# Attention kernel on one core: the transpose that feeds the row of maxima runs at key tile 1 instead of key tile 0, with a 128-column stationary operand

## The chip, the cores and the metric

One Trainium2 chip, one of its cores. The metric is the device time of one execution in microseconds, the median over several runs.

## The reference

For each of 16 sequences of 1024 tokens with 512 channels the reference adds a masked self-attention to its input:

```python
q = xt @ Wq.T                                   # 8 heads of 64 channels
scores = scale * jnp.einsum('bhqd,bhkd->bhqk', qh, qh)
logits = (scores * cmask + (1.0 - cmask) * NEG) * rmask
attn = jax.nn.softmax(logits, axis=-1)
ctx = jnp.einsum('bhqk,bhkd->bhqd', attn, qh)
out = ctx.transpose(0, 2, 1, 3).reshape(B, T, D) @ Wo.T
x = x + transpose(out)
```

Queries, keys and values are the same matrix. About half of the tokens are masked. A masked query has the same logit for every key, so its output is the mean of all tokens times both weight matrices.

## The kernel before

The kernel gathers the unmasked tokens of a sequence (a "batch" b) into NT = 5 tiles of R = 108 rows (the form "small", taken here), and does dense attention on them. For every head the 540 queries stand in two halves of H = 270 columns, and the keys in five tiles. The loops run over 16 batches (a hardware loop over pairs of batches for most of them), in each over 8 heads h, and in each over 5 key tiles k. I call one pass of the innermost loop the step (h, k). Each of the five engines has its own program with the same loops, and waits on semaphores for the others.

TensorE (`batch`, `misc`) does in the step (h, k), in this order:

1. `max_scores` 2k of head h+2 (line 1029): scores of one half of the queries against one tile, whose maxima are needed to subtract them before the exponential;
2. `scores` of head h, tile k (lines 1044 and 1047);
3. part 0 of the step's small jobs;
4. `max_scores` 2k+1 of head h+2;
5. `times_values` of the tile before (line 1057, 64 stationary columns a half);
6. part 1 of the small jobs.

The small jobs are set by tables of steps at the head of the file: V (transposes of the values), L (row sums, line 1151), proj and out (projections, line 1090), xT (transposes of the next batch's tokens, line 1102, at (3,1) to (3,4) and (4,0)), and mT. They write into two PSUM banks in turn: a job waits until the job two before it has left its bank (`bank_left`). Long jobs are split between the two parts; xT and mT are done in part 1, V and L in part 0.

The way of the maxima of head h+1 is: VectorE reduces each `max_scores` (`reduce_max`, line 831, two PSUM banks in turn), folds them into the column `mcol` at the end of head h-1 (line 836), TensorE transposes `mcol` (job mT, line 1146) in head h, ScalarE copies the result to `mrow` (`max_row`, line 655), and SyncE writes it by DMA as one row of the operands of head h+1 (`put_max_row`, line 431). TensorE's `scores` of head h+1 wait for it.

SyncE's queue (`batch` in the sync block) has two things to do in head h, in this order: `put_max_row` for head h+1, and `copy_operands` for head h+3, six DMAs (line 425) that build the operands `ops` of that head. The first `max_scores` of head h+3, at the start of head h+1, wait for these six.

ScalarE does in each step the two exponentials (line 702), then its share of the step's jobs in the order of the table (for xT the copy of line 605 and the masking of the next tile, line 675), then at key tile 1 of odd heads `ctx_high` (line 667), which feeds `ctx_low` on VectorE (line 867, at key tile 2), which the job out at step (1,2) waits for.

Of the kernel before, what the change touches and what calls it, by code (L numbers as in the profile page):

```python
# [19 lines left out]
P = 128  # L20
F32 = mybir.dt.float32
# [4 lines left out]
ALU = mybir.AluOpType  # L26
# [15 lines left out]
XT_AT = [(3, 1), (3, 2), (3, 3), (3, 4), (4, 0)]  # L42
OUT_AT = [(1, 2), (1, 4), (2, 0), (2, 2), (2, 3)]
XBAR_AT, W_AT = (7, 1), (7, 3)
RECIPROCAL_AT = [(2, 1), (2, 1), (3, 0), (3, 1)]
SCALE_AT = [(4, 1), (0, 0)]
CTX_LOW_AT = (2, 0)
# [25 lines left out]
def misc_jobs(form, has_prev, has_next):  # L73

    NT = form.NT
    table = {(h, k): [] for h in range(HEADS) for k in range(NT)}
    steps = list(table)
    for h in range(HEADS):  # L80
        if h % 2 == 1 and (h < 7 or has_next):
            table[h, V_AT[0]].append(("V", ((h + 1) // 2, 0)))
            table[h, V_AT[1]].append(("V", ((h + 1) // 2, 1)))
        if h > 0 or has_prev:
            table[h, 2].append(("L", h - 1))
    if has_prev:
        for k, at in enumerate(out_steps(form)):
            table[at].append(("out", k))

    for at, pair in zip(PROJ_AT, ((2, 1), (3, 0), (3, 1), (4, 0), (4, 1), (5, 0), (5, 1), (6, 0))):  # L90
        if at < (4, 0) or has_next:
            table[at].append(("proj", pair))
    if has_next:
        for k in range(NT):
            table[XT_AT[k] if form.split else (3, k)].append(("xT", k))
        table[XBAR_AT].append(("xbar", 0))
        table[W_AT].append(("w", 0))
    for h in range(HEADS - 1 + has_next):
        table[h, 0].append(("mT", h + 1))
    for jobs in table.values():  # L100

        assert all(name not in TWO_PARTS for name, _ in jobs[:-2])
    return table
# [126 lines left out]
def attention_kernel(nc, x_rows, mask_t, wq, wqT, woT, out_rows, B, T, D):  # L230
# [6 lines left out]
    with ExitStack() as ctx:  # L237
# [6 lines left out]
        def sem(name):  # L244
            return ctx.enter_context(nc.semaphore(name))
# [37 lines left out]
        out_step, out_done, rsum_done = sem("out_step"), sem("out_done"), sem("rsum_done")  # L283
        recip_step, xlo_done, ctx_lo_done = sem("recip_step"), sem("xlo_done"), sem("ctx_lo_done")

        wlo_done = sem("wlo_done")
        pacc_step, idx_copied, tail_added = sem("pacc_step"), sem("idx_copied"), sem("tail_added")

        sp_passed, pool_passed = sem("sp_passed"), sem("pool_passed")
# [21 lines left out]
        for f, t in zip(forms, tensors):  # L311
            own = ExitStack()

            def keep(name, shape, dt, stack=own, t=t, f=f):
                t[name] = sb(f"{f.name}_{name}", shape, dt, stack)
# [38 lines left out]
            keep("xsum", [P, D], F32)  # L354
            keep("xv", [P, f.NA, D], F32)
            keep("mxp", [P, 2, f.NT, 2], F32)
            keep("mcol", [P, 2, f.NT], F32)
            keep("mrow", [f.NT, 2, f.R], F32R)
            if f.split:
                for name in ("wqT_hi", "wqT_lo", "woT_hi", "woT_lo"):  # L360
# [93 lines left out]
        def _(pool):  # L454
# [14 lines left out]
            def body(f, t, plan):  # L469
# [84 lines left out]
                pool.wait_ge(idx_made, 2)  # L554
                if f.split:
                    pool.wait_ge(wlo_done, 2)
                nc.gpsimd.memset(t["ops"][DK:P, :, OPX, :].bitcast(F32), 0.0).then_inc(ops_cleared, 1)
                nc.gpsimd.memset(t["ops"][DK:P, :, OPY, :].bitcast(F32), 0.0).then_inc(ops_cleared, 1)
                pool.wait_ge(ops_cleared, 2)
# [173 lines left out]
        def _(dve):  # L733
# [25 lines left out]
            def body(f, t, plan):  # L759
# [68 lines left out]
                def reduce_max(s, h, m):  # L828

                    dve.wait_ge(mx_ready, 2 * NT * s + m + 1)  # L830
                    nc.vector.tensor_reduce(t["mxp"][:R, h % 2, m // 2, m % 2:m % 2 + 1], MX[m % 2][:R, 0:H], AX.X,  # L831
                                            ALU.max).then_inc(mx_red, 1)
                    if m == 2 * NT - 1:
                        dve.wait_ge(mx_red, 2 * NT * (s + 1))
                        at_least(dve, mT_ready, s - 1)
                        nc.vector.tensor_reduce(t["mcol"][:R, h % 2, :], t["mxp"][:R, h % 2], AX.X, ALU.max,
                                                negate=True).then_inc(mcol_done, 1)

                def job(name, arg, bank, b, par, s):
# [134 lines left out]
        def _(pe):  # L974
# [11 lines left out]
            def body(f, t, plan):  # L986
# [107 lines left out]
                def job(name, arg, bank, before, b, par, s, chunks=range(KD)):  # L1094
# [35 lines left out]
                    elif name == "V":  # L1130
# [11 lines left out]
                                                    start=False, stop=True)  # L1142
                        last.then_inc(v_ready, 1)
                    elif name == "mT":
                        pe.wait_ge(mcol_done, s + 1)
                        nc.tensor.transpose(mb[:NT, 0:R], t["mcol"][:R, arg % 2, :], ident[:R, :R]).then_inc(mT_ready, 1)
                    elif name == "L":

                        pe.wait_ge(pacc_step, (NT - 1) * (s + 1))
                        for half in range(2):  # L1150
                            last = nc.tensor.matmul(mb[DK * half:DK * half + DK, 0:H], ones64[:R, :],  # L1151
                                                    t["Pacc"][:R, arg % HEADS % f.NA, half, :], start=True, stop=True)
                        last.then_inc(l_ready, 1)
                    elif name == "out":
                        if chunks[0] == 0:

                            pe.wait_ge(ctx_lo_done if f.split else ctx_done, (PAIRS if f.split else HEADS) * b)
                        for c in chunks:
                            last = product(mb[:R, 0:D], "ctxT", t["ctxT"],
                                           (slice(None), c, tile_cols(arg)),  # L1160
                                           "woT", woT_sb, (slice(None), c, slice(None)), c)
                        if c == KD - 1:
                            last.then_inc(out_ready, 1)
# [77 lines left out]
```

## Time and profile before

| what | value |
|---|---|
| median of 3 runs | 1997.83 us (1994.7 to 2000.62) |
| span of the profiled execution | 2000.9 us |
| PE (TensorE matmul) | 1806.9 us busy, 90% |
| DVE (VectorE) | 1486.2 us, 74% |
| POOL (GpSimd) | 1203.5 us, 60% |
| ACT (ScalarE) | 946.8 us, 47% |
| mean granted TensorE clock | 0.956 of full speed |
| chain that ended last | PE 50%, DVE 24%, issue 16%, ACT 4%, POOL 3%, DMA 1% |

The profiled execution's span of 2000.9 us lies 0.15% above the median of the runs. The busy shares are means over stages in which different engines are late: TensorE is nearly always busy, and in some steps waits for VectorE.

### The profile page before, as it was taken

How to read it: one execution, taken by the hardware profiler on the slowest of the kernel's cores; microseconds unless marked ns; L12 is line 12 of the kernel's file. 1: busy time of each engine (PE TensorE's matmuls, PEld its weight loads, DVE VectorE, ACT ScalarE, POOL GpSimd, SP SyncE). 2: the span in 40 equal slices, each digit the busy share in tenths (PEclk: the TensorE clock that was granted, in tenths of full speed). 3: DMA queues.
4: the chain of work that ended last, by engine and by line, in shares of the span. 5: the costliest groups of instructions: out<-in, count | busy, mean ns of one | idle time of the engine just before them, and what ended most of it. 6: DMA issues, size and time to landing. Idle time of an engine off the chain costs nothing.

```text
span 2000.9 us, 39654 instructions
## 1 busy us (share of the span) xinstructions
PE 1806.9 (90%) x10636; PEld 1184.8 (59%) x10636; DVE 1486.2 (74%) x2839; ACT 946.8 (47%) x2311; POOL 1203.5 (60%) x1030
## 2 busy tenths in 40 slices
PE   6599989999999999989999999999989999998995
PEld 4456656656556565656656666566656656665663
DVE  4359687787958778697876968668696787869774
ACT  1246455454535545354544535445454554536452
POOL 5265666647566574666646566564766656576653
PEclk8689999999989999999989999889999999999997
DMA  3233343434324342343424334243343424334320
GB/s 106 50 98 91 95 98 81 122 68 115 89 71 113 69 124 65 102 101 75 113 67 115 84 91 99 64 113 78 102 101 77 111 68 117 86 93 105 78 71 24
DMA packets 93863, 179.69 MB, mean 90 GB/s; under 512 B 24704, under 2 KB 24832, under 8 KB 93632
## 3 DMA queue, kind: packets, MB, share of 16 engines
q1 hardware_dynamic: 64448, 109.71, 23.8%
q0 software_dynamic: 29184, 67.17, 12.1%
q8 instruction: 112, 1.84, 0.4%
q14 instruction: 119, 0.97, 0.2%
HBM read 36.77 MB, written 33.55 MB: 35 GB/s over the span
## 4 chain that ended last, share of the span: by engine, by line
PE 50%; DVE 24%; issue 16%; ACT 4%; POOL 3%; DVEq 1%; SPq 1%; DMA 1%; ACTq 0%; POOLq 0%
PE misc L1090 20%; PE ctx_psum L1057 9%; DVE small_mxp L831 9%; PE max_scores L1029 7%; DVE small_xsum L826 5%; DVE small_ctx L880 4%; PE scores L1044 3%; PE scores L1047 3%; PE misc L1116 3%; PE misc L1151 2%; DVE small_rsum L862 2%; DVE small_xcT_lo L854 1%; DVE small_ctxT_lo L867 1%; ACT small_H L633 1%; ACT small_Q L630 1%
## 5 line engine op out<-in xcount | busy, mean ns | idle before, releaser
L831 DVE TENSOR_REDUCE small_mxp<-max_scores 108x1 f32<-108x270 f32 x1280 | 530.8, 423 | 378.2 <-PE max_scores L1029 359.1
L539 POOL TENSOR_TENSOR small_Pacc<-small_Pacc,small_Pt 108x540 f32<-108x540 f32 x384 | 547.1, 1425 | 370.7 <-ACT small_Pt L702 366.7
L702 ACT ACTIVATE small_Pt<-scores,small_kbias 108x270 f32<-108x270 f32 x1280 | 551.0, 483 | 404.9 <-PE scores L1047 371.8
L1029 PE MATMUL max_scores<-small_ops 128*108 128x270 f32 x1280 | 457.8, 359 | 126.7 <-DVE small_mxp L831 118.4
L1057 PE MATMUL ctx_psum<-small_Pt,small_V 108*64 108x270 f32 x2560 | 448.3, 425 | 1.9 <-ACT small_ctxraw L661 1.9
L1029 PEld LDWEIGHTS max_scores<-small_ops 128*108 128x108 f32 x1280 | 225.5, 176 | 357.7 <-DVE small_mxp L831 250.3
L862 DVE RECIPROCAL small_rsum<-small_rsum 128x67 f32<-128x67 f32 (+1 forms) x512 | 271.2, 551 | 5.5 <-ACT small_rsum L648 4.2
L539 POOL TENSOR_TENSOR small_Pacc<-small_Pt 108x540 f32<-108x540 f32 x128 | 178.4, 1394 | 158.0 <-ACT small_Pt L702 156.4
L1044 PE MATMUL scores<-small_ops 128*108 128x270 f32 x1280 | 272.9, 295 | 0.0
L1047 PE MATMUL scores<-small_ops 128*108 128x270 f32 x1280 | 269.4, 292 | 0.0
L880 DVE TENSOR_TENSOR small_ctx<-small_rsum,small_ctxraw 64x270 f32<-64x270 f32 x256 | 242.8, 948 | 9.7 <-issue 0.3
L491 POOL DMA_INDIRECT small_xg<-x_rows,small_idx_cur x160 | 166.1, 1038 | 103.9 <-POOL small_idx_cur L484 69.7
L498 POOL DMA_INDIRECT out_rows<-small_xg,small_idx_cur x160 | 162.8, 1017 | 93.1 <-DVE small_xg L915 51.5
L630 ACT COPY small_Q<-misc 128x270 f32<-128x270 f32 x128 | 49.2, 384 | 334.7 <-PE misc L1090 327.8
L1044 PEld LDWEIGHTS scores<-small_ops 128*108 128x108 f32 x1280 | 196.5, 178 | 11.2 <-issue 4.9
L1057 PEld LDWEIGHTS ctx_psum<-small_Pt,small_V 108*64 108x64 f32 x2560 | 134.0, 137 | 113.3 <-issue 57.9
L1047 PEld LDWEIGHTS scores<-small_ops 128*108 128x108 f32 x1280 | 196.0, 177 | 0.0
L826 DVE TENSOR_TENSOR small_xsum<-small_xsum,small_xg 108x512 f32<-108x512 f32 (+1 forms) x128 | 180.6, 1411 | 2.0
L1090 PE MATMUL misc<-small_xcT,small_wqT_hi 128*128 128x270 f32 x512 | 163.8, 320 | 1.9 <-DVE small_xcT_lo L854 1.3
L1090 PE MATMUL misc<-small_xcT_lo,small_wqT_hi 128*128 128x270 f32 x512 | 150.8, 295 | 0.0
L1090 PE MATMUL misc<-small_woT_hi,small_ctxT 128*108 128x512 f32 x320 | 135.9, 425 | 16.3 <-DVE small_ctxT_lo L867 16.3
L1090 PE MATMUL misc<-small_xcT,small_wqT_lo 128*128 128x270 f32 x512 | 150.2, 293 | 0.0
(104 smaller groups left out, 2184.4 us busy)
## 6 DMA issues: line engine op xcount, KB each, us to landing
small_ops<-small_H SPq DMA_DIRECT2D x512, 135.0 KB, 3.2
small_ops<-small_L SPq DMA_DIRECT2D x256, 135.0 KB, 3.4
small_xg<-x_rows,small_idx_cur POOLq DMA_INDIRECT x160, 4.2
out_rows<-small_xg,small_idx_cur POOLq DMA_INDIRECT x160, 3.4
small_ops<-small_mrow SPq DMA_DIRECT2D x128, 2.1 KB
wq_sb<-wq SPq DMA_DIRECT2D x1, 1024.0 KB, 5.4
woT_sb<-woT SPq DMA_DIRECT2D x1, 1024.0 KB, 7.8
wqT_sb<-wqT SPq DMA_DIRECT2D x1, 1024.0 KB, 9.8
```

The lines of the kernel that those rows point to most:

```text
L491: nc.gpsimd.indirect_dma_start(out=t["xg"][:r, par, k, :], out_offset=None, in_=x_rows, in_offset=bass.IndirectOffsetOnAxis(ap=t["idx_cur" ...
L539: nc.gpsimd.tensor_tensor(acc, other, t["Pt"][:R, p0], ALU.add).then_inc(pacc_step, 1)
L702: nc.scalar.activation(t["Pt"][:R, (NT * h + k) % f.NP, half, :], ST[(2 * (NT * h + k) + half) % 3][:R, 0:H], ACT.Exp, bias=t["kbias"][:R, ...
L826: nc.vector.tensor_tensor(acc[:r], other, t["xg"][:r, par, k, :], ALU.add).then_inc(xsum_step, 1)
L831: nc.vector.tensor_reduce(t["mxp"][:R, h % 2, m // 2, m % 2:m % 2 + 1], MX[m % 2][:R, 0:H], AX.X, ALU.max).then_inc(mx_red, 1)
L862: nc.vector.reciprocal(t["rsum"][:, cols], t["rsum"][:, cols]).then_inc(recip_step, 1)
L880: last = nc.vector.tensor_tensor(t["ctx"][pr:pr + DK, h // 2 % 2, cols] if f.split else t["ctxT"][pr:pr + DK, h // 2, cols], t["rsum"][r0: ...
L1029: nc.tensor.matmul(MX[m % 2][:R, 0:H], ops[:, OPA, tile_cols(m // 2)], ops[:, OPB, half_cols(m % 2)], start=True, stop=True).then_inc(mx_r ...
L1044: nc.tensor.matmul(banks[half][:R, 0:H], ops[:, OPA, tile_cols(k)], ops[:, OPB, half_cols(half)], start=True, stop=False)
L1047: nc.tensor.matmul(banks[half][:R, 0:H], ops[:, OPY, tile_cols(k)], ops[:, OPX, half_cols(half)], start=False, stop=True).then_inc(s_ready, 1)
L1057: last = nc.tensor.matmul(CT[DK * half:DK * half + DK, 0:H], t["V"][:R, (h // 2) % 2, k, DK * (h % 2):DK * (h % 2) + DK], t["Pt"][:R, (NT ...
L1090: last = nc.tensor.matmul(out, lefts[a][left_at], rights[z][right_at], start=(c == 0 and i == 0), stop=(c == KD - 1 and i == 2))
```

## The change

The job mT is put into the table at key tile 1 instead of key tile 0, on all engines that read the table. `mcol` is widened from NT columns to 128, of which the last 123 are cleared once at the start by GpSimd; the transpose takes all 128 as its stationary operand and writes 128 rows of the bank instead of 5. ScalarE still reads the first 5. TensorE waits in addition for the clearing.

```diff
+MT_AT = 1
@@ misc_jobs
     for h in range(HEADS - 1 + has_next):
-        table[h, 0].append(("mT", h + 1))
+        table[h, MT_AT].append(("mT", h + 1))
@@ tensors
-            keep("mcol", [P, 2, f.NT], F32)
+            keep("mcol", [P, 2, P], F32)
@@ gpsimd, before the loops
+                nc.gpsimd.memset(t["mcol"][:, :, NT:], 0.0).then_inc(mcol_padded, 1)
+                pool.wait_ge(mcol_padded, 1)
@@ vector, reduce_max
-                        nc.vector.tensor_reduce(t["mcol"][:R, h % 2, :], t["mxp"][:R, h % 2], AX.X, ALU.max,
+                        nc.vector.tensor_reduce(t["mcol"][:R, h % 2, 0:NT], t["mxp"][:R, h % 2], AX.X, ALU.max,
@@ tensor, job
                     elif name == "mT":
+                        pe.wait_ge(mcol_padded, 1)
                         pe.wait_ge(mcol_done, s + 1)
-                        nc.tensor.transpose(mb[:NT, 0:R], t["mcol"][:R, arg % 2, :], ident[:R, :R]).then_inc(mT_ready, 1)
+                        nc.tensor.transpose(mb[:, 0:R], t["mcol"][:R, arg % 2, :], ident[:R, :R]).then_inc(mT_ready, 1)
```

## Rows read from the trace of the kernel before

**Rows 1.** Waits: engine, line, who ended it: us in total, times, longest.

```profile
PE max_scores L1029 <- DVE small_mxp L831: 118.4, 209, 5.1
...
PE misc L1090 <- DVE small_ctxT_lo L867: 16.3, 16, 4.9
```

**Rows 2.** Groups by line and shape: busy us, mean ns | idle before, releasers.

```profile
L1102 PEld LDWEIGHTS misc<-ident,small_xv 108*128 108x128 f32 x320 | 34.3, 153 | 46.6 <-issue 29.0 <-ACT small_xv L675 12.8 <-DVE small_xcT_lo L854 4.9
...
L1146 PE MATMUL misc<-ident,small_mcol 108*5 108x108 f32 x128 | 33.0, 258 | 4.2 <-DVE small_xcT_lo L854 3.5 <-DVE small_mcol L836 0.7
...
L1146 PEld LDWEIGHTS misc<-ident,small_mcol 108*5 108x5 f32 x128 | 10.7, 83 | 45.5 <-issue 39.2 <-DVE small_xcT_lo L854 4.3 <-DVE small_mcol L836 1.0
```

**Rows 3.** Timeline (start, duration), TensorE, batch 7, heads 3 and 4.

```profile
968.94 0.26 PE L1146 MATMUL misc<-ident,small_mcol 108*5 108x108 f32 x1
...
973.34 0.68 PE L1151 MATMUL misc<-small_Pacc,ones 108*64 108x270 f32 x4
...
979.65 0.35 PE L1029 MATMUL max_scores<-small_ops 128*108 128x270 f32 x1
...
981.75 0.26 PE L1146 MATMUL misc<-ident,small_mcol 108*5 108x108 f32 x1
981.78 0.36 PE L1029 MATMUL max_scores<-small_ops 128*108 128x270 f32 x1
```

**Rows 4.** Timeline, ScalarE, same head 3.

```profile
969.32 0.24 ACT L655 CAST small_mrow<-misc 5x108 fp32r<-5x108 f32 x1 [0.66 <-PE misc L1146]
...
973.31 0.72 ACT L675 ACTIVATE small_xv<-small_xg,small_valid 108x512 f32<-108x512 f32 x1
...
973.93 0.63 ACT L667 CAST small_ctxT<-small_ctx 128x540 fp32r<-128x540 f32 x1
```

**Rows 5.** Timeline, SyncE, same head: the last of the six copies.

```profile
973.96 0.60 SPq L425 DMA_DIRECT2D small_ops<-small_L  x1
```

**Rows 6.** Window just after that transfer (us, TensorE clock, DMA share, GB/s).

```profile
978.00:979.00 1.00, 1.00 0.02 8
```

**Rows 7.** All DMAs into the operands, from issue to landing.

```profile
DMA to landing us min/median/max: 2.2/3.2/6.4
```

**Rows 8.** Timeline, VectorE, in head 3 and at the start of head 4.

```profile
973.44 0.61 DVE L854 TENSOR_TENSOR small_xcT_lo<-misc,small_xcT 128x432 fp32r<-128x432 f32 x1
...
980.58 0.42 DVE L831 TENSOR_REDUCE small_mxp<-max_scores 108x1 f32<-108x270 f32 x1
```

**Rows 9.** Timeline, batch 7: ScalarE in head 0, TensorE in heads 0 and 1.

```profile
919.68 0.24 ACT L655 CAST small_mrow<-misc 5x108 fp32r<-5x108 f32 x1 [0.26 <-PE misc L1146]
...
922.61 0.37 PE L1029 MATMUL max_scores<-small_ops 128*108 128x270 f32 x1
...
929.54 0.38 PE L1029 MATMUL max_scores<-small_ops 128*108 128x270 f32 x1
```

**Rows 10.** Window after the transfer of head 0 (clock, DMA share, GB/s).

```profile
927.00:928.00 1.00, 1.00 0.02 4
```

**Rows 11.** Timeline, batch 7, head 1: ScalarE, VectorE, TensorE.

```profile
934.52 0.68 ACT L667 CAST small_ctxT<-small_ctx 128x540 fp32r<-128x540 f32 x1
...
935.67 1.20 DVE L867 TENSOR_TENSOR small_ctxT_lo<-small_ctx,small_ctxT 128x540 fp32r<-128x540 f32 x1
...
934.79 0.37 PE L1029 MATMUL max_scores<-small_ops 128*108 128x270 f32 x1
...
937.01 0.45 PE L1090 MATMUL misc<-small_woT_hi,small_ctxT 128*108 128x512 f32 x1 [0.75 <-DVE small_ctxT_lo L867]
```

**Rows 12.** Windows over head 0 of batches 4 and 5, head 3 of 10 and 11: us, PE busy, clock, DMA.

```profile
556.60:572.93 16.33, 14.59 (x67) 0.69 0.24 55
680.10:691.84 11.74, 10.74 (x70) 1.00 0.31 72
1329.93:1346.76 16.83, 15.55 (x79) 0.70 0.44 116
1448.65:1461.77 13.12, 11.46 (x78) 1.00 0.53 133
```

More of the change, by code:

```diff
@@ L284, in attention_kernel @@
         recip_step, xlo_done, ctx_lo_done = sem("recip_step"), sem("xlo_done"), sem("ctx_lo_done")
-        wlo_done = sem("wlo_done")
+        wlo_done, mcol_padded = sem("wlo_done"), sem("mcol_padded")
         pacc_step, idx_copied, tail_added = sem("pacc_step"), sem("idx_copied"), sem("tail_added")
```

## The prediction

> **What bounds the kernel now.** I read the page's busy shares first: TensorE is busy for 90% of the span, no other engine for more than 74%, and the chain that ended last lies on PE for 50% and on DVE for 24%. So TensorE's queue sets the pace, and what can hurt is what makes it wait. The table of waits says what does so today: VectorE's reductions of the maxima, 118 us in 209 waits, and at one place in each batch `ctx_low`, 16.3 us in 16 waits [rows 1]. SyncE's copies cost TensorE almost nothing. The reader is to see that both the transpose mT and the copies are off this path, and that the question is with how much room. For that I read the timeline of one whole batch (batch 7), and there four ends: where mT runs, where its `mrow` is made, when the last of the six copies behind it has landed, and when TensorE first needs them.
>
> **The transpose itself.** In 128 executions it is 33.0 us of matmul and 10.7 us of weight load, 258 and 83 ns each [rows 2], but what it takes of TensorE's time is the step to the next start: `max_scores` starts 0.03 us after it where VectorE is not late (981.75 to 981.78) [rows 3]. At key tile 0 TensorE mostly waits for VectorE afterwards, so taking it away there gives 0 to 0.03 us. At key tile 1 little waits behind it, and it costs its full price. That price with 128 columns is not in the trace; the nearest is the weight load of the 128-column transposes, 153 ns against 83 [rows 2]. So 0.03 us if the load stays covered, 0.10 if the difference of 0.07 is added, and nothing speaks for less. I take 0.045 us over the 7 heads other than head 3 in 16 batches: 112 x 0.045 = 5 us, with ends 3 and 11.
>
> The Trainium skill ("TensorE: Matmul & The Clock Gate", section "LDWEIGHTS (loading the stationary operand)") makes a load as long as its number of columns at 1.2 GHz. That would be an estimated 0.10 us more for 128 columns than for 5, and an estimated 13 us for all; the trace has a difference of 0.07 us, and by that the upper end stands.
>
> **The edits with one answer.** The clearing of 123 columns on GpSimd happens once before the loops, where SyncE and TensorE wait for the projections anyway: 0, at most 1 us. The wait on it is met for good after that and stands with two others before a weight load that starts late anyway: 0. VectorE's fold and ScalarE's copy are as long as before.
>
> **The copies behind mT.** This is the large term. On SyncE `copy_operands` stands behind `put_max_row`, which waits for `mrow`. So moving mT moves six DMAs too.
>
> Head 3 first. There ScalarE has, at key tile 1, the xT copy and the masking (from 973.31) to do ahead of the moved `max_row`, because xT stands before mT in the table. The place that comes free is where `ctx_high` starts now, 973.93; with 0.24 us `mrow` is then done at 974.17 instead of 969.32 + 0.24 = 969.56, which is 4.61 us later [rows 4]. Now the last copy is issued at 973.96 [rows 5] and the engines are quiet again by 978.0 [rows 6], 1.65 us before TensorE's first `max_scores` of head 4 at 979.65 [rows 3]. Moved by 4.61 they land at 982.61, and TensorE stands for 2.96 us. Of this a part is hidden: VectorE is behind at that place and reduces that `max_scores`, which ends at 979.65 + 0.35 = 980.00, only from 980.58 [rows 8]. That takes 0.58 off: 2.4 us. Head 3 has xT in 15 of the 16 batches: 36 us. How long a copy takes is the uncertain part: here 4.0 us from the last issue to landing, in all between 2.2 and 6.4 [rows 7], since the gathers share the engines. With 2.2 the term is 15 x 0.6 = 9 us, with 6.4 it is 15 x 4.8 = 72. I take the row of the place itself.
>
> Head 0: `mrow` is done at 919.92. Moved, mT starts close before the `max_scores` at 922.61, and `mrow` follows 0.38 + 0.24 us behind it (968.94 to 969.32 [rows 3, 4]), at 923.23: 3.31 us later [rows 9]. The copies are through by 927.0 [rows 10] and would be by 930.3, where TensorE wants them at 929.54 [rows 9]: 0.8 us, of which I estimate half to fall into the wait for VectorE that follows. Four of the even batches have a longer head 0 with room enough. 11 x 0.35 = 4 us. Heads 5 and 6 are about as long as head 0 and reach their limit by the same reckoning; I give them 3 us together, with ends 0 and 10. Heads 1, 2, 4 and 7 last clearly longer in the timeline and have the room.
>
> **What else stands behind mT.** In head 1 `ctx_high` on ScalarE, now from 934.52 for 0.68 us, comes to stand behind the moved `max_row`. With mT just before 934.79, `mrow` is done at about 935.38 and `ctx_high` at 936.06, so `ctx_low` begins 0.4 us after its 935.67 of now. The projection at 937.01 already waits for it by 0.75 us [rows 11]. So 0.4 us lies wholly on the path, in 15 batches: 6 us, and nothing covers it. In heads 5 and 7 no such job waits at that place. In head 3 a second effect is hidden: the row sums (973.34 [rows 3]) now have xT two jobs before them and wait for its bank, which VectorE's `xcT_lo` leaves at 974.05 [rows 8]. These 0.7 us come before the stall at head 4, which is shorter by the same, so they are not added.
>
> **TensorE's clock.** Head 0 takes 11.74 us in batch 5 at a granted clock of 1.00, and 16.33 in batch 4 at 0.69; head 3 takes 13.12 us in batch 11 at 1.00 and 16.83 in batch 10 at 0.70 [rows 12]. So where the clock falls to its lower level (1.2 GHz) for part of a head, that head is some 3.7 us longer, part of it the pause itself. Waits of 3 us at the start of head 4 may bring it down more often. I take 9 us (one more fall of a third of that size in half of the batches would be 9), with ends 0 and 15 x 3.7 = 56.
>
> **The sum.** 36 + 4 + 3 + 6 + 5 + 9 = 63 us on the profiled execution's 2000.9 us gives a span of 2064. The runs' median lies 3 us under that span, so 1997.8 + 63 = 2061 us.
>
> **The rivals.**
>
> 1. The copies come quickly. Shifted, they may meet fewer gathers; with 2.2 us instead of 4.0 head 3 costs 9 us, heads 0, 5 and 6 nothing, and 6 + 5 remain: 1997.8 + 20 = 2018 us. For it speaks the median of 3.2 us [rows 7], against it that gathers of the next batch run through all of head 3 and 4. Chance 0.17.
> 2. The clock falls in every batch after the new wait: 54 + 56 = 110, 2108 us. For it speak the heads of [rows 12], against it that waits of 1 us at the same place go without a fall in half of the batches. Chance 0.13.
> 3. Faster: the clock falls less often. In head 0 of four even batches TensorE pauses behind mT at key tile 0 and then runs at the lower level. If the transpose no longer stands ahead of that pause and the level stays up, four heads save up to 4.6 us and head 3 of batch 10 another 3.7: 22 us [rows 12]. It decides only if the copies land with their room of 1.65 us kept, that is, if the queue moves by less than this; then 1997.8 - 22 + 11 = 1987 us. Against it: the move of 4.61 us follows from the order on ScalarE. Chance 0.05.
> 4. The narrow operand costs a change of layout that the wide one saves. If the next `max_scores` had to wait for mT's end, 0.26 us, there would be 128 x 0.23 = 29 us to win, and the sum would be 2032 us. The row speaks against it: the next start comes after 0.03 us [rows 3]. Chance 0.03.
> 5. Nothing to be measured: the move is absorbed everywhere, and even head 1's 6 us are. Chance 0.05.
>
> The Trainium skill ("TensorEngine Tiling (Array Packing)", section "Key Properties") says that a change of the tiling mode drains TensorE, which is the rule behind the fourth; by this trace there is no drain behind mT.
>
> **How the numbers follow.** The forecast has 0.57. It and the first two rivals are slower. A measurement of this kernel tells about 0.3%, 6 us, from no change. Slower by more than that: the forecast, the first two rivals and the fourth, 0.90, less 0.02 for the low end of the first; within it 0.05 of the fifth and 0.01 from there; faster 0.05 of the third and the other 0.01. The range reaches from below the first rival to near the second: 2012 to 2106 us.
>
> **What would show it.** In the profile after: a new wait of `max_scores` for the copies of L, some 3 us each, at the start of head 4 in 15 batches and shorter ones at heads 1, 6 and 7; the wait for `ctx_low` grown from 16 us to about 22; `mrow` in head 3 only after the masking; mT's weight load near 150 ns with the next start within 0.1 us. If the copies' wait stays under 10 us in total, the large term is wrong, and with it the prediction; if the clock's mean moves from 0.956 by more than 0.01, the clock term is.

## The result and the profile after

The changed kernel takes 2028.7 us (median of 4 runs, 2024.6 to 2033.9); the kernel before, run beside it, 1998.2 us. The ratio is 1.0164 with a 95% interval of 1.0140 to 1.0189: 33 us slower, between 28 and 38. I had forecast 2061 us and a range from 2012 to 2106. The profiled execution has a span of 2022.8 us, 21.9 us over that of before, whose own span lay above the times of all its runs; so what follows accounts for some 22 of the 33 us, execution against execution.

First the page of the changed kernel: the busy shares, the granted clock in 40 slices, and the chain that ended last.

```profile
PE 1804.9 (89%) x10636; PEld 1197.5 (59%) x10636; DVE 1426.0 (70%) x2839; ACT 945.2 (47%) x2311; POOL 1209.3 (60%) x1031
...
PEclk8689989999989989989999999999998999999998
...
PE 59%; DVE 13%; issue 11%; SPq 5%; DMA 4%; ACT 3%; POOL 2%; DVEq 1%; ACTq 0%; POOLq 0%
```

TensorE's busy time is the same as before. SyncE's queue and the DMAs are on the chain now, with 9% of the span, where they had 1% each. VectorE is busy for 60 us less, though it does the same work: this was in none of my terms, and is the key to the rest.

Then the waits of the changed kernel (engine, line, who ended it: us, times, longest), beside [rows 1]:

```profile
PE max_scores L1032 <- DVE small_mxp L834: 80.8, 136, 5.0
PE max_scores L1032 <- DMA small_ops<-small_L: 62.0, 39, 4.4
...
PE misc L1155 <- DVE small_xcT_lo L857: 9.1, 15, 0.8
PE misc L1093 <- issue: 8.2, 12, 0.7
PE misc L1093 <- DVE small_ctxT_lo L870: 7.3, 4, 4.9
```

`max_scores` waits 62 us for copies, a wait of which the kernel before has 3 us. Row sums wait 15 times, some 0.6 us each, for the bank that xT of head 3 holds. Against them the wait for VectorE's reductions is 38 us shorter. The waits of the projection at (1,2) are 15.5 us together, and were 16.3.

The timeline of the changed kernel at the place of the large term, batch 7, heads 3 and 4, which answers to [rows 3 to 6] and [rows 8]:

```profile
986.71 0.72 ACT L678 ACTIVATE small_xv<-small_xg,small_valid 108x512 f32<-108x512 f32 x1
...
987.33 0.22 ACT L658 CAST small_mrow<-misc 5x108 fp32r<-5x108 f32 x1
987.46 0.64 ACT L670 CAST small_ctxT<-small_ctx 128x540 fp32r<-128x540 f32 x1
...
991.94 0.60 SPq L426 DMA_DIRECT2D small_ops<-small_L  x1
...
996.30 0.37 PE L1032 MATMUL max_scores<-small_ops 128*108 128x270 f32 x1 [2.60 <-DMA small_ops<-small_L]
```

The row of maxima is made only behind the masking, just ahead of `ctx_high`, as worked out. Head 3 starts at 978.90 here and at 966.53 before. The last of the six copies is issued at 991.94, and TensorE stands for 2.60 us at the start of head 4. I had put 2.96.

What the steps add up to is best seen by heads. This table has the mean length of each head in us over the 15 batches that have a next one, from the start of its first `max_scores` to that of the next head, for both kernels and for four of the runs below.

| head | before | after | move alone | head 3 alone | small adds | third sum later |
|---|---|---|---|---|---|---|
| 0 | 12.52 | 13.18 | 13.00 | 12.43 | 11.91 | 12.34 |
| 1 | 18.13 | 17.91 | 17.61 | 18.15 | 18.16 | 18.11 |
| 2 | 18.26 | 18.04 | 18.04 | 18.27 | 18.12 | 18.26 |
| 3 | 13.67 | 17.09 | 17.12 | 17.22 | 13.78 | 13.40 |
| 4 | 16.02 | 13.73 | 13.76 | 14.04 | 14.18 | 14.86 |
| 5 | 12.02 | 12.11 | 12.14 | 12.21 | 11.51 | 11.95 |
| 6 | 11.49 | 11.48 | 11.18 | 11.37 | 11.37 | 11.53 |
| 7 | 15.53 | 15.39 | 15.36 | 15.56 | 15.59 | 15.52 |

(The wait at the start of a head stands in the length of the head before.) Head 3 is 3.42 us longer, and head 4 gives 2.29 of it back. All others together are 0.14 us a batch longer. (Two expectations below have 3.3 and 2.0 for the pair; these were means that took in the last, shorter batch.)

### The profile page after: what moved, and what is told of

Same layout as the page of the kernel before. It is cut to its first block, busy times and chain, and to the rows that moved or that the text cites. A ratio compares the mean times of both kernels' runs of the same rounds, so it can differ in the third digit from the quotient of the medians.

```text
span 2022.8 us, 39656 instructions
## 1 busy us (share of the span) xinstructions
PE 1804.9 (89%) x10636; PEld 1197.5 (59%) x10636; DVE 1426.0 (70%) x2839; ACT 945.2 (47%) x2311; POOL 1209.3 (60%) x1031
## 4 chain that ended last, share of the span: by engine, by line
PE 59%; DVE 13%; issue 11%; SPq 5%; DMA 4%; ACT 3%; POOL 2%; DVEq 1%; ACTq 0%; POOLq 0%
PE misc L1093 22%; PE ctx_psum L1060 12%; PE max_scores L1032 7%; DVE small_mxp L834 6%; PE scores L1047 4%; PE scores L1050 4%; DMA small_ops<-small_L 4%; SPq L426 4%; PE misc L1119 3%; PE misc L1155 3%; DVE small_ctx L883 3%; PE misc L1105 2%; DVE small_xsum L829 1%; PE misc L1150 1%; ACT small_H L636 1%
## 5 line engine op out<-in xcount | busy, mean ns | idle before, releaser
L1060 PE MATMUL ctx_psum<-small_Pt,small_V 108*64 108x270 f32 x2560 | 455.6, 433 | 2.6 <-ACT small_ctxraw L664 1.9
L1032 PEld LDWEIGHTS max_scores<-small_ops 128*108 128x108 f32 x1280 | 238.3, 186 | 342.1 <-DVE small_mxp L834 196.5
L1047 PE MATMUL scores<-small_ops 128*108 128x270 f32 x1280 | 279.0, 301 | 0.0
L1050 PE MATMUL scores<-small_ops 128*108 128x270 f32 x1280 | 274.4, 297 | 0.0
L883 DVE TENSOR_TENSOR small_ctx<-small_rsum,small_ctxraw 64x270 f32<-64x270 f32 x256 | 227.6, 889 | 9.6 <-issue 0.3
L1047 PEld LDWEIGHTS scores<-small_ops 128*108 128x108 f32 x1280 | 200.8, 182 | 13.2 <-issue 4.9
L1050 PEld LDWEIGHTS scores<-small_ops 128*108 128x108 f32 x1280 | 200.4, 181 | 0.0
L1093 PE MATMUL misc<-small_woT_hi,small_ctxT 128*108 128x512 f32 x320 | 135.9, 425 | 15.5 <-issue 8.2
L829 DVE TENSOR_TENSOR small_xsum<-small_xsum,small_xg 108x512 f32<-108x512 f32 (+1 forms) x128 | 137.0, 1071 | 2.0
```

Source lines behind the costliest of these rows:

```text
L883: last = nc.vector.tensor_tensor(t["ctx"][pr:pr + DK, h // 2 % 2, cols] if f.split else t["ctxT"][pr:pr + DK, h // 2, cols], t["rsum"][r0: ...
L1032: nc.tensor.matmul(MX[m % 2][:R, 0:H], ops[:, OPA, tile_cols(m // 2)], ops[:, OPB, half_cols(m % 2)], start=True, stop=True).then_inc(mx_r ...
L1047: nc.tensor.matmul(banks[half][:R, 0:H], ops[:, OPA, tile_cols(k)], ops[:, OPB, half_cols(half)], start=True, stop=False)
L1050: nc.tensor.matmul(banks[half][:R, 0:H], ops[:, OPY, tile_cols(k)], ops[:, OPX, half_cols(half)], start=False, stop=True).then_inc(s_ready, 1)
L1060: last = nc.tensor.matmul(CT[DK * half:DK * half + DK, 0:H], t["V"][:R, (h // 2) % 2, k, DK * (h % 2):DK * (h % 2) + DK], t["Pt"][:R, (NT ...
L1093: last = nc.tensor.matmul(out, lefts[a][left_at], rights[z][right_at], start=(c == 0 and i == 0), stop=(c == KD - 1 and i == 2))
```

## Experiments

My theory was: the move delays SyncE's six copies, and head 3 carries the loss because ScalarE has xT to do first. Its rivals: the wide operand, the clock, and the many smaller waits. No run holds the clock fixed; what the rows say of it stands in the last part. After the trace there was a second question: why head 4 is shorter.

### The wide operand alone

```diff
-MT_AT = 1
+MT_AT = 0
```

> The wide operand alone, the transpose left at key tile 0. If the loss comes from the copies queued behind the transpose, this is as fast as the kernel before (within 4 us), with a weight load of 138 ns instead of 83 and no wait of max_scores for the copies over the 3 us of before. If the wide operand itself costs TensorE time, it is slower by up to 128 x 0.1 = 13 us. If the narrow operand had cost a change of layout, it is faster by up to 29 us.

Measured: ratio 1.0014 (0.9988 to 1.0039), no difference. The groups of the transpose's weight load, first in this run and then in the run with the move alone, which comes next (line, engine, operands, count | busy, mean ns | idle before):

```profile
L1150 PEld LDWEIGHTS misc<-ident,small_mcol 108*128 108x128 f32 x128 | 17.8, 139 | 46.7 <-issue 42.2 <-DVE small_xcT_lo L857 3.4
```

```profile
L1150 PEld LDWEIGHTS misc<-ident,small_mcol 108*5 108x5 f32 x128 | 11.1, 87 | 52.1 <-issue 40.7 <-ACT small_V L643 10.6 <-DVE small_xcT_lo L857 0.8
```

The wide load is 52 ns longer, and at key tile 0 VectorE's lateness hides it. There was no change of layout to save either.

### The move alone

```diff
-                        nc.tensor.transpose(mb[:, 0:R], t["mcol"][:R, arg % 2, :], ident[:R, :R]).then_inc(mT_ready, 1)
+                        nc.tensor.transpose(mb[:NT, 0:R], t["mcol"][:R, arg % 2, 0:NT], ident[:R, :R]).then_inc(mT_ready, 1)
```

> The transpose at key tile 1, its operand 5 columns wide as before. If the move alone makes the loss, this is slower than the kernel before by the same 27 to 33 us as the changed kernel, or up to 8 us less, and max_scores waits for the copies by some 60 us. If the wide operand makes a good part of it, the loss is below 20 us.

Measured: 2015.2 us beside 1993.9, ratio 1.0099 (1.0065 to 1.0132): 20 us slower, between the two cases that were expected. Its largest new wait is again that for copies, 59.8 us. So the move makes the greater part, and the width, harmless at key tile 0, adds to it at key tile 1. The two timelines say how much it costs directly, the move alone first and then the changed kernel:

```profile
1011.89 0.26 PE L1150 MATMUL misc<-ident,small_mcol 108*5 108x108 f32 x1
1011.93 0.36 PE L1032 MATMUL max_scores<-small_ops 128*108 128x270 f32 x1
```

```profile
1001.31 0.31 PE L1150 MATMUL misc<-ident,small_mcol 108*128 108x108 f32 x1
1001.40 0.35 PE L1032 MATMUL max_scores<-small_ops 128*108 128x270 f32 x1
```

From the transpose to the next start the narrow one takes 30 ns and the wide one 84 (medians of 112, all behind `times_values`). So the width is 112 x 0.054 = 6 us. The ratios of the two kernels differ by 13 us, and by my estimate that is good to some 8 us either way; what lies between 6 and 13 is not settled.

### The copies ahead of the row of maxima

```diff
+                        if h < HEADS - 3 or has_next:
+                            copy_operands(s + 3, h + 3)
                         if h < HEADS - 1 or has_next:
                             put_max_row(s + 1, h + 1)
-                        if h < HEADS - 3 or has_next:
-                            copy_operands(s + 3, h + 3)
```

> The changed kernel with SyncE's two tasks in a head exchanged: the six copies for head h+3 are issued ahead of the row of maxima of head h+1, so that they no longer stand behind the transpose. If the copies behind the transpose are the cause, the wait of max_scores for them goes from 62 us to under 3 us and the time comes back to within 10 us of the kernel before. If the pauses behind VectorE, the wait for ctx_low or the transpose's own time at key tile 1 are the cause, it stays over 15 us slower. The rows of maxima are issued behind six copies then, some 4 us after the head's start at the earliest, which should cost nothing as they are wanted a head later.

> The kernel before with the same exchange on SyncE, the control for the run above. TensorE waits for copies by only 2.8 us in the kernel before, so by the theory of the copies this is within 4 us of it. If instead the time at which the copies run, against the gathers and VectorE's work, matters by itself, it moves by more than 6 us either way.

Measured, on the changed kernel: 2003.0 us beside 1993.9, ratio 1.0039 (1.0022 to 1.0057), within the 10 us. The waits are

```profile
PE max_scores L1032 <- DVE small_mxp L834: 125.9, 172, 5.4
PE max_scores L1032 <- issue: 13.8, 12, 1.7
...
PE misc L1155 <- DVE small_xcT_lo L857: 8.6, 12, 0.8
```

Of the wait for copies 2.2 us in one place are left, and some 25 us of the 33 are gone with it. The wait for VectorE is back at 126 us: the two are not independent. The 13.8 us put down to `issue` are waits for which the profile shows no releaser; 11.1 of them stand in step (4,1). The control was a miss: on the kernel before the same exchange costs 12 us (2005.7 us, ratio 1.0060, 1.0038 to 1.0082). Head 0 is 0.57 us a batch longer there, all eight heads together 1.0; by the timeline that of head 0 comes at the turn of the hardware loop, in the even batches. First VectorE in the kernel before, batch 8, then the same place in the control, with SyncE's copies:

```profile
1037.69 0.44 DVE L831 TENSOR_REDUCE small_mxp<-max_scores 108x1 f32<-108x270 f32 x1 [1.58 <-issue]
```

```profile
1038.18 0.48 SPq L425 DMA_DIRECT2D small_ops<-small_H  x1
1038.71 0.59 SPq L425 DMA_DIRECT2D small_ops<-small_L  x1
1039.36 3.31 SPq L425 DMA_DIRECT2D small_ops<-small_H  x3
...
1042.80 0.44 DVE L831 TENSOR_REDUCE small_mxp<-max_scores 108x1 f32<-108x270 f32 x1 [2.25 <-issue]
```

There VectorE waits for nothing that a semaphore tells, 1.58 us before and 2.25 where six copies run at that moment. In all five turns TensorE's pause grows from 1.5 to 1.7 us to 2.2 to 2.5, and the clock falls behind each of them, in the kernel before behind four. That the engines' instructions come late there because the copies are in their way fits this, but I did not test it. It would be a reason for part of the 8 and 12 us by which the exchanged kernels stay slower.

### Head 3 alone, and all but head 3

```diff
-        table[h, MT_AT].append(("mT", h + 1))
+        table[h, MT_AT if h == 3 else 0].append(("mT", h + 1))
```

> The wide operand everywhere, but the transpose moved to key tile 1 in head 3 alone. The changed kernel's trace has head 3 longer by 3.3 us and head 4 shorter by 2.0 us in a batch. If head 3's move makes both, the same two numbers stand here, and the whole is 15 x 1.3 = 20 us over the kernel before, up to 5 us more or less. If head 4's gain comes from its own moved transpose, head 4 stays at 15.6 us and the whole is some 45 us slower.

> The wide operand everywhere, the transpose moved in all heads but head 3. By the trace's heads the others sum up to about -0.6 + 0.7 = 0.1 us in a batch without the pair of heads 3 and 4, so this is 0 to 10 us slower than the kernel before; the wait of max_scores for the copies is 62 - 38 = 24 us or less. If the many small waits at heads 0, 5 and 6 carry the loss, it is 15 us or more.

Measured: head 3 alone 2027.7 us beside 1993.3, ratio 1.0162 (1.0133 to 1.0191): 32 us, the same as the whole change, and above the 15 to 25 expected from the trace. All but head 3 (`h != 3` in the same line): 2003.0, ratio 1.0042 (1.0018 to 1.0066), 8 us with 28.5 us of waits for copies, of which at most 24 were expected. So one transpose of eight makes most of the loss: by itself as much as all eight, and without it a quarter stays. In the table head 3 alone gives +3.55 and -1.98 us, near the pair of the changed kernel, with head 4's own transpose left in place. So head 4 gives back because of the stall in front of it, not because of its own move.

### The row of maxima ahead of the masking

```diff
-                            for name, arg, bank, before in table[h, k]:
+                            for name, arg, bank, before in sorted(table[h, k], key=lambda j: j[0] == "xT"):
```

> The changed kernel, where ScalarE in head 3 makes the row of maxima ahead of the xT copy and the masking of the next tile, not behind them. If the place on ScalarE makes 1.3 of the 4.6 us by which the copies move there, the wait of max_scores at the start of head 4 falls from 2.5 us a batch to about 1.3, and the whole becomes 5 to 15 us faster than the changed kernel, less what head 4 then no longer gives back. If the order on ScalarE did nothing, it is as slow as the changed kernel.

Measured: 2010.7 us, ratio 1.0075 (1.0050 to 1.0100), against 1.0164 some 18 us faster than the changed kernel, above the 5 to 15 expected. The wait at the start of head 4 falls from 38.0 to 29.3 us in all, 0.6 a batch, which is half of what I had expected. Head 3 is 16.4 us and head 4 14.1. The two traces differ by 8 us only, so the size of this gain is less certain than its sign. Part of it may be the clock's: it was at the lower level for 137 us inside the loop, and for 164 in the changed kernel.

### Why head 4 is shorter

In the kernel before VectorE does three sums of tokens in head 4. The timeline of batch 7 there, VectorE and GpSimd:

```profile
983.60 0.69 DVE L826 TENSOR_TENSOR small_xsum<-small_xg 108x512 f32<-108x512 f32 x1
985.07 2.26 DVE L826 TENSOR_TENSOR small_xsum<-small_xsum,small_xg 108x512 f32<-108x512 f32 x1
987.61 2.46 DVE L826 TENSOR_TENSOR small_xsum<-small_xsum,small_xg 108x512 f32<-108x512 f32 x1
...
985.42 1.36 POOL L539 TENSOR_TENSOR small_Pacc<-small_Pt 108x540 f32<-108x540 f32 x1
986.95 1.19 POOL L491 DMA_INDIRECT small_xg<-x_rows,small_idx_cur  x1 [0.18 <-POOL small_Pacc L539]
988.16 1.35 POOL L539 TENSOR_TENSOR small_Pacc<-small_Pacc,small_Pt 108x540 f32<-108x540 f32 x1
```

The same operation takes 0.69 us by itself and 2.3 to 2.5 beside GpSimd. In the changed kernel, the same three:

```profile
998.51 0.69 DVE L829 TENSOR_TENSOR small_xsum<-small_xg 108x512 f32<-108x512 f32 x1
...
1000.73 0.68 DVE L829 TENSOR_TENSOR small_xsum<-small_xsum,small_xg 108x512 f32<-108x512 f32 x1
...
1001.48 1.36 POOL L540 TENSOR_TENSOR small_Pacc<-small_Pt 108x540 f32<-108x540 f32 x1 [2.48 <-ACT small_Pt L705]
...
1001.68 1.71 DVE L829 TENSOR_TENSOR small_xsum<-small_xsum,small_xg 108x512 f32<-108x512 f32 x1
```

Their mean in head 4 is 1.02 us against 1.81. While TensorE stands, VectorE works off what it was behind with, and then does two of the sums before GpSimd's first add of the head. Two runs take GpSimd's two kinds of work away from head 4, in the kernel before: the first issues the gathers in head 3, the second leaves out most of head 4's row sums.

```diff
-            table[steps[GATHER_TAIL_FROM + i]].append(("gather", NT + i))
+            table[steps[GATHER_TAIL_FROM + i // 2]].append(("gather", NT + i))
```

> The kernel before, the five gathers of the last tiles issued two a key tile in head 3, so that GpSimd issues none in head 4. The theory is that head 4 gives 2 us back in the changed kernel since VectorE's sums of tokens no longer run beside GpSimd's work, which makes them 1.8 us long instead of 0.7 to 1.0. Then the sums in head 4 fall here too, from 1.81 us to 1.3 or less, and head 4 gets shorter by 1 to 2 us a batch, up to 30 us in all if head 3 does not pay for it. If head 4 is short in the changed kernel only because the stall lets the other engines catch up, the sums may fall but head 4 stays within 0.4 us of 15.6.

```diff
-                    nc.gpsimd.tensor_tensor(acc, other, t["Pt"][:R, p0], ALU.add).then_inc(pacc_step, 1)
+                    n = 2 if h == 4 else f.H
+                    nc.gpsimd.tensor_tensor(acc[:, :, :n], other[:, :, :n], t["Pt"][:R, p0, :, :n],
+                                            ALU.add).then_inc(pacc_step, 1)
```

> The kernel before, where GpSimd's adds of the row sums in head 4 take 2 of 270 columns; most of head 4's row sums is left out, all else is computed. Moving the gathers out of head 4 had left VectorE's sums of tokens there at 1.75 us. If they are long because GpSimd's adds run beside them, they fall here from 1.81 us to about 0.9 (what is left are the gathers), and head 4 goes from 15.6 to about 13.5 us, as it is in the changed kernel: some 30 us faster in all. If the adds do not matter, sums and head 4 stay within 0.2 and 0.4 us.

Measured: without the gathers the sums stay at 1.75 us, head 4 at 16.11, and the whole is 10 us slower (1.0051, 1.0026 to 1.0077): the guess on the gathers was wrong. The clock was lower in these runs (median 0.951 against 0.962 beside them), which goes with the 10 us. With the adds of head 4 cut short the whole is 35 us faster (0.9822, 0.9791 to 0.9853), head 4 is 14.18 us long, and the sums are at their bare length, even beside a gather. VectorE and GpSimd in that run:

```profile
960.97 0.69 DVE L828 TENSOR_TENSOR small_xsum<-small_xg 108x512 f32<-108x512 f32 x1
962.44 0.68 DVE L828 TENSOR_TENSOR small_xsum<-small_xsum,small_xg 108x512 f32<-108x512 f32 x1
963.38 0.70 DVE L828 TENSOR_TENSOR small_xsum<-small_xsum,small_xg 108x512 f32<-108x512 f32 x1
...
960.46 1.01 POOL L491 DMA_INDIRECT small_xg<-x_rows,small_idx_cur  x1 [0.18 <-issue]
...
963.36 0.94 POOL L491 DMA_INDIRECT small_xg<-x_rows,small_idx_cur  x1 [0.18 <-POOL small_Pacc L540]
```

So it is GpSimd's adds, not its gathers, that make VectorE's sums long. Other engines hardly wait for these adds: in the kernel before ScalarE does so for 20.4 us in all, none of it in head 4, and TensorE for 1.1, so the gain does not come by that way. In the kernel before, each of the two long sums of head 4 ends 0.55 us after an add does: 985.42 + 1.36 = 986.78 and 985.07 + 2.26 = 987.33; 988.16 + 1.35 = 989.51 and 987.61 + 2.46 = 990.07. The adds keep their own 1.35 us. All 30 long sums of head 4 in the trace end 0.55 to 0.57 us after an add.

The Trainium skill ("SBUF — State Buffer", section "SBUF: two separate sides") says that VectorE and GpSimd share a pair of ports as an exclusive lock: a VectorE operation with two SBUF inputs and a GpSimd operation that reads SBUF don't run together, the one that starts second blocks until the first is done. The trace agrees with the blocking. It does not agree on who comes first, as far as the records' starts can be trusted: both long sums are recorded as starting ahead of the add (by 0.35 and 0.55 us), and it is the sums that wait.

### The move only in the heads with room

```diff
-        table[h, MT_AT].append(("mT", h + 1))
+        table[h, MT_AT if h in (1, 2, 4, 7) else 0].append(("mT", h + 1))
```

> The narrow operand, the transpose moved only in heads 1, 2, 4 and 7, where the copies behind it had 2.9 to 6 us of room on average before they were wanted. If only the lack of room costs time, max_scores waits for copies by under 8 us in all and the kernel is within 4 us of the kernel before. If the moved transpose costs by itself (ctx_low in head 1, VectorE's waits), it is 6 us or more slower; if heads 1, 2 and 7, which are 0.2 to 0.6 us shorter in the run with the move alone, owe this to their own move, it is up to 12 us faster.

The operand is 5 columns wide here, as in the run with the move alone. Measured: 1998.3 us beside 1997.2, ratio 1.0019 (1.0000 to 1.0038). There are 5 waits for copies, 9.6 us together, all in or ahead of the first batch and in the last. In the others the four heads that I had said have the room do have it, and to move their transposes gains nothing measurable either.

### The sums of head 4 placed otherwise

If head 4 of the changed kernel is shorter because the sums miss the adds, the table of the sums alone should give that without the stall. Two versions of the kernel before, with no other edit:

```diff
-SUM_AT = [(4, 0, 1), (4, 1, 0), (4, 1, 1), (5, 1, 0), ...
+SUM_AT = [(4, 0, 1), (4, 0, 1), (4, 1, 0), (5, 1, 0), ...
```

> The kernel before, nothing left out: VectorE's second sum of tokens in head 4 is done right behind the first, at key tile 0, and the third a half key tile earlier, so that two of the three run before GpSimd's first add of the head. If only running beside the adds makes them long, the mean of the three falls from 1.81 to about 1.0 us and head 4 gets 1 to 1.5 us shorter a batch, less up to 0.7 us as a reduction of the maxima now stands behind the second sum: 5 to 20 us faster. If the reduction's delay outweighs it, no faster.

```diff
-SUM_AT = [(4, 0, 1), (4, 1, 0), (4, 1, 1), (5, 1, 0), ...
+SUM_AT = [(4, 0, 1), (4, 1, 0), (4, 3, 0), (5, 1, 0), ...
```

> The kernel before, nothing left out: the third sum of tokens in head 4 at key tile 3, where TensorE has a long projection, not at key tile 1. The sum may stay 1.7 to 2.5 us long, but TensorE's wait for VectorE at key tile 2 (head 4 has 5.6 us there against 4.2 with the adds left out) should go: 5 to 20 us faster. If VectorE is late at key tile 3 as well, the wait only moves, and the time stays within 4 us.

The first gained nothing: ratio 1.0009 (0.9988 to 1.0029). The sums were shorter (mean of the three 1.14 us), but head 4 stayed at 16.01 us. Two things ate the gain. In batch 7, with the clock at 1.00 in both kernels, step (4,2) falls from 5.78 to 4.57 us and step (4,1) grows from 2.92 to 3.59, since two sums in a row stand ahead of the next reduction: head 4 is 14.85 us long instead of 15.43. And the clock fell in head 4 in 10 of the 15 batches of this trace, where it did in 5 of before; these heads take 15.7 us and more. The trace is one of the slower executions (2006 us, the median is 1996), so the second is clear in kind and not in size.

The second gained: 1981.1 us beside 1996.2, ratio 0.9933 (0.9910 to 0.9956), 13 us faster than the kernel before and some 47 faster than the changed one. Head 4 is 14.86 us long, 1.16 less, which is 17 us in 15 batches; it is step (4,2) that shrinks, from 5.80 to 4.99, and the rest lies in the steps behind. The clock fell in head 4 in 2 batches instead of 5; with head 4 at 1.00 in both kernels batch 7 has 14.36 us against 15.43. VectorE in that run, batch 7:

```profile
972.05 0.69 DVE L826 TENSOR_TENSOR small_xsum<-small_xg 108x512 f32<-108x512 f32 x1
973.52 2.28 DVE L826 TENSOR_TENSOR small_xsum<-small_xsum,small_xg 108x512 f32<-108x512 f32 x1
...
980.11 0.63 DVE L826 TENSOR_TENSOR small_xsum<-small_xsum,small_xg 108x512 f32<-108x512 f32 x1
```

One sum of 2.3 us stays where two were. The third takes 0.63 us. GpSimd's add beside it is the one that is long here:

```profile
980.08 1.86 POOL L539 TENSOR_TENSOR small_Pacc<-small_Pacc,small_Pt 108x540 f32<-108x540 f32 x1 [2.09 <-ACT small_Pt L702]
982.92 1.34 POOL L539 TENSOR_TENSOR small_Pacc<-small_Pacc,small_Pt 108x540 f32<-108x540 f32 x1 [0.98 <-ACT small_Pt L702]
```

Its 0.5 us cost nothing: the next add waits for ScalarE anyway, 0.98 us.

## Why the prediction was right or wrong

The direction, the place and the mechanism were right; the size was 33 us instead of 63. What failed is the give-back: I took 0.58 us of the stall to be hidden, and 2.29 came back. By the steps:

- **The queue, ScalarE first (right).** The row of maxima in head 3 is made behind the masking, the six copies come after it, and TensorE waits for them at the start of head 4. Head 3's move alone gives the whole loss, and the six copies put ahead of the row take most of it back.
- **The stall of head 3 (size nearly right, in part by luck).** 2.96 us worked out, 2.60 at that place in batch 7. Two misses offset each other there. The last copy is issued 991.94 - 978.90 = 13.04 us into head 3 where it was 973.96 - 966.53 = 7.43: 5.61 us later, and not 4.61. And TensorE itself reaches the end of head 3 in 17.40 - 2.60 = 14.80 us instead of 13.12, 1.68 later, where I had counted 0.7 for the row sums and nothing for a lower clock. The waits in front of head 4 come to 38.0 us, 36.2 in 13 of the 15 batches and 1.8 in the last batch; in batches 1 and 5, with head 3 at 0.70 of the clock, there is none. In front of heads 1, 2, 3, 5, 6 and 7 they are 7.0, 2.0, 3.0, 1.8, 3.1 and 4.5 us, and 2.5 ahead of the first batch. Head 3 is 3.42 us longer: 2.41 for the copies, about 0.6 for the row sums, which wait for the bank, and the rest fits the lower clock.
- **What is hidden of it (the step that failed).** I took 0.58 us, the lateness of VectorE at that moment. Head 4 gave back 2.29. In this kernel VectorE went on through the stall with what was queued, and that queue holds two-input operations that GpSimd's adds stretch from 0.69 to 2.3 us. Once it had caught up, they fell beside fewer adds: the three sums of head 4 take 3 x (1.81 - 1.02) = 2.4 us less a batch. That they are the cause is shown by the run with the short adds, which has a short head 4 without a stall; how much of the 2.29 us is theirs and how much plain catching up was not separated. So heads 3 and 4 cost 3.42 - 2.29 = 1.13 us a batch, 17 us in 15 batches, where I had 36. In the last batch, where I had nothing, the same two heads are 3.2 us longer. I had read from the trace that the copies come late, and not what the late place does to the engine that is the limit behind it.
- **Head 0 and the projection of head 1 (one right, one wrong).** I had 4 and 6 us. The wait for copies behind head 0 is 7.0 us in all; head 0 is 0.66 us a batch longer and head 1 is 0.22 shorter, together 0.44, which is 7 in 15 batches. In head 1 the start of `ctx_low` came 0.28 us later, where I had 0.4, but it took 0.85 us instead of 1.20 and ended no later, 2.01 us behind the first `max_scores` of its step against 2.08. Rows from the changed kernel, batch 7:

```profile
947.36 1.37 POOL L540 TENSOR_TENSOR small_Pacc<-small_Pt 108x540 f32<-108x540 f32 x1
947.65 0.24 ACT L658 CAST small_mrow<-misc 5x108 fp32r<-5x108 f32 x1 [0.56 <-PE misc L1150]
947.80 0.64 ACT L670 CAST small_ctxT<-small_ctx 128x540 fp32r<-128x540 f32 x1
948.47 0.85 DVE L870 TENSOR_TENSOR small_ctxT_lo<-small_ctx,small_ctxT 128x540 fp32r<-128x540 f32 x1 [0.33 <-ACT small_ctxT L670]
```

  It is the same sharing: the add ends at 948.73 and `ctx_low` at 949.32, 0.59 us behind it; begun later, it meets less of the add. My "nothing covers it" left out that the operation's length depends on its place. The wait at (1,2) stayed at 16 us; I had said 22.
- **Heads 5, 6 and 7.** 3 us worked out, none found (+0.09, -0.01 and -0.14 us a batch), inside the ends of 0 and 10.
- **The transpose.** 0.045 us each worked out. From the last matmul before it to the next `max_scores` it is 0.321 us where no transpose stands between, 0.351 with the narrow one and 0.406 with the wide one (medians of 111): 0.085 us, some 9 us in 112 places for the 5 worked out, inside my ends of 3 and 11. The wide load is 56 ns longer at key tile 0 (139 against 83) and 61 at key tile 1 (148 against 87). No rival of a layout change was seen: the padding by itself changed nothing. The Trainium skill's rule ("TensorE: Matmul & The Clock Gate", section "LDWEIGHTS (loading the stationary operand)"), by which I had given 13 us, would make the load an estimated 103 ns longer; the measurement decides against it here.
- **The clock (term too small).** Its mean fell from 0.956 to 0.941. That is more than the 0.01 that I had named as the sign that my clock term is wrong. The time at the lower level inside the loop grew from 96 us in 16 stretches to 164 in 31. These are the windows over head 3 and head 4 of batch 7, before (us, then busy of each engine, clock, DMA share, GB/s):

```profile
966.53:979.65 13.12, 11.46 (x78) 7.22 (x77) 11.21 (x27) 10.36 (x24) 9.70 (x11) 1.00 0.51 133
979.65:995.08 15.43, 12.85 (x87) 8.67 (x85) 14.62 (x25) 7.84 (x20) 10.30 (x9) 1.00 0.52 119
```

  And after, with head 4 of batch 5 as the third:

```profile
978.90:996.30 17.40, 12.73 (x78) 8.08 (x77) 12.21 (x29) 11.54 (x26) 12.82 (x13) 0.90 0.45 118
996.30:1009.82 13.52, 13.52 (x83) 9.52 (x83) 10.62 (x22) 6.80 (x18) 7.47 (x7) 0.87 0.40 112
...
755.99:768.39 12.40, 12.17 (x87) 8.63 (x85) 10.63 (x23) 7.74 (x20) 9.04 (x7) 1.00 0.49 127
```

  In head 4 of batch 7 TensorE is busy without a gap at 0.87 of the clock, and VectorE's 14.62 us became 10.62: behind the stall TensorE sets the pace of this head, so the lower clock lies on the path. In batches 1 and 5 the clock had fallen early in head 3 instead, which was no longer for it (17.1 and 17.3 us at 0.70, 17.4 in batch 7 at 0.90), and stood at 1.00 in head 4, which took 12.15 and 12.40 us. In the other 13 batches, at 0.78 to 0.88, it took 13.5 to 14.8, the mean of all being 13.73. The lower clock thus costs some 1.5 us a batch in head 4, an estimate from two heads at 1.00. In the kernel before the mean is 16.02 and the ten heads at 1.00 have 15.40: 0.6 us. So the clock takes some 12 us more in head 4 than before, where I had 9 us for all heads, and with the clock up head 4 would have given back over 3 us. The runs point the same way: over the 70 runs of the kernel before that stood beside the experiments, a mean clock that is 0.001 higher goes with a time that is 1.1 us shorter (0.955 to 0.971, correlation -0.86). The changed kernel's clock is some 0.02 lower, an estimated 20 us, though this counts with the clock the pauses in front of its falls. No run kept the clock up with the stall in place, so a split of the 33 us stays an estimate.

- **The rivals.** Copies that come quickly (2018 us) would have shown no wait at heads 1 and 6 and a small one at head 4; the table of waits has 62 us. A fall of the clock in every batch (2108) did come: behind each of the 13 new waits of 2.3 to 4.4 us in front of head 4, and in batches 1 and 5 in head 3. It costs some 1.7 us where it meets head 4, and not the 3.7 of that rival, whose price held the pause as well. A clock that falls less often is not there. The result lies between the first rival and the forecast because of the give-back, which was in no case of mine.

By heads the account closes: 1.13 us for heads 3 and 4 and 0.14 for the six others are 1.27 a batch, 19 us in 15 batches, and the last batch has 3, where the two spans differ by 22. The ratio says 33 (28 to 38); the span of before lay above its median and that of after below its own, which is most of the rest.

What the stall gave back, 2.29 us a batch or 34 in 15 batches, is time in which VectorE had been late. The kernel with the third sum moved gains 13 us there, without the stall.

## What to carry to other kernels

When a step is moved, follow not only who waits longer, but what the engine behind that wait does meanwhile: if the stretch after it is bound by another engine, much of the stall comes back there, and the way that it comes back can show an improvement that needs no stall. On VectorE, cost an operation with two inputs from SBUF by what GpSimd does at that moment, not by its mean. When a new wait is put in front of TensorE, read the granted clock behind it head by head: it costs where TensorE then sets the pace, and next to nothing where TensorE waits anyway. And before a DMA queue is given a late item to wait for, look at what is queued behind it; here six copies stood behind a row of 540 numbers.

## What the runs showed of the hardware

- A VectorE addition of 108x512 in fp32 takes 0.69 us alone and 2.26 to 2.46 beside GpSimd additions of 1.35, and in each of these cases ends 0.55 us after the add. Beside GpSimd's issue of an indirect DMA (0.94 to 1.0 us) it keeps its 0.69. To cut the adds of one head of eight to 2 of their 270 columns was worth 35 us.
- At the turn of the hardware loop VectorE stands for 1.4 to 1.6 us with no semaphore to wait for, and for 2.2 to 2.6 where six copies between SBUF buffers run at that time. The cause was not tested.
- The weight load of a 128-column stationary operand (fp32, 108 partitions) takes 139 to 148 ns and that of a 5-column one 83 to 87; behind `times_values` the transposes are followed by the next `max_scores` after 84 and 30 ns. At key tile 0, where TensorE mostly waits for VectorE, no loss by it was measured (ratio 1.0014, 0.9988 to 1.0039).
- Behind each of 13 pauses of TensorE of 2.3 to 4.4 us in front of head 4 the granted clock stood at its lower level (1.2 GHz) for part of the head. The head takes 12.15 and 12.40 us at a mean of 1.00 and 13.5 to 14.8 at 0.78 to 0.88.
